# Three pairs of PSUM banks for the edge counts, and slot sums, block sums and turned features in the four partition groups of one bank

## What is computed

```python
def sage_conv(x, edge_index, W_l, b_l, W_r, num_segments):
    src, dst = (edge_index[0], edge_index[1])
    agg = jax.ops.segment_sum(x[src], dst, num_segments=num_segments)
    return agg @ W_l.T + b_l + x @ W_r.T
h = jax.nn.relu(sage_conv(x, edge_index, W_l_in, b_l_in, W_r_in, n))
out = sage_conv(h, edge_index, W_l_out, b_l_out, W_r_out, n)
x = _layernorm(x + out)
```

## Time and profile before

| | us |
|---|---|
| median of three executions | 5961.28 (5933.37 to 5972.20) |
| the profiled execution, its own time | 5973.71 |
| its span in the profile | 5971.6 |
| PE, ACT, DVE, POOL busy | 4194.8, 2238.6, 2727.6, 3172.5 |

### The profile page before, as it was taken

How to read it: one execution, slowest core, us unless ns; L and a number is a source line. 1 busy time by engine, 2 the same in 40 slices (tenths; PEclk the granted TensorE clock), 3 DMA queues, 4 the chain that set the end, 5 groups by cost and what they waited for, 6 DMA issues and landing times. The chain is left out here.

```text
span 5971.6 us, 92359 instructions
## 1 busy us (share of the span) xinstructions
PE 4194.8 (70%) x31126; PEld 3201.6 (54%) x31126; DVE 2727.6 (46%) x6953; ACT 2238.6 (37%) x5687; POOL 3172.5 (53%) x3030
## 2 busy tenths in 40 slices
PE   4777777777867777778757577676666676666656
PEld 2444444444445555544557566566565665566646
DVE  6635444444211111234322355655556556466586
ACT  2555555555300000156200045445454454444520
POOL 4645545555145555553066566565555655565645
PEclk9898888888667777888555567676677766667776
DMA  2323343343257777400122223333333333333332
GB/s 83 144 99 141 141 155 150 149 155 147 91 208 256 255 251 257 153 9 7 46 53 51 59 70 85 79 85 85 76 84 79 79 89 74 80 86 81 85 84 64
DMA packets 324619, 660.29 MB, mean 111 GB/s; under 512 B 124556, under 2 KB 208454, under 8 KB 316232
## 3 DMA queue, kind: packets, MB, share of 16 engines
q1 hardware_dynamic: 230246, 581.33, 27.6%
q0 software_dynamic: 92160, 74.67, 7.7%
q10 hardware_dynamic: 1896, 0.12, 0.0%
HBM read 393.69 MB, written 262.14 MB: 110 GB/s over the span
## 5 line engine op out<-in xcount | busy, mean ns | idle before, releaser
L1667 POOL DMA_INDIRECT gath<-fs_scratch,src_idx x1568 | 1615.4, 1030 | 1158.1 <-issue 459.9
L681 POOL DMA_INDIRECT gath<-in_x,src_idx x720 | 767.4, 1066 | 724.9 <-PE sum_x_ps_g L791 442.1
L1716 PE MATMUL ps_e<-fdw,scratch 128*128 128x66 f32 x3136 | 789.7, 337 | 395.8 <-issue 195.1
L729 ACT ACTIVATE scratch<-sum_x_ps_c 128x800 bf16<-128x800 f32 x932 | 763.0, 836 | 669.6 <-PE sum_x_ps_c L748 469.0
L1796 ACT ACTIVATE scratch<-scratch,bias,weight 128x32 f32<-128x32 f32 x2608 | 931.2, 403 | 55.1 <-DVE bias L1869 47.8
L1718 PE MATMUL ps_e<-gath,ident 128*128 128x66 f32 x3136 | 785.8, 336 | 151.4 <-issue 150.7
L681 POOL DMA_INDIRECT gath<-y_scratch,src_idx x592 | 597.2, 1009 | 543.1 <-PE sum_y_ps_g L791 353.2
L1716 PEld LDWEIGHTS ps_e<-fdw,scratch 128*128 128x128 f32 x3136 | 639.6, 249 | 454.5 <-issue 419.2
L1779 ACT ACTIVATE scratch<-ps_o 128x512 f32<-128x512 f32 x394 | 227.9, 596 | 1446.9 <-remote 844.8
L748 PE MATMUL sum_x_ps_c<-e_tab,scratch 128*128 128x400 bf16 x1864 | 541.2, 378 | 320.1 <-ACT scratch L729 171.2
L1718 PEld LDWEIGHTS ps_e<-gath,ident 128*128 128x128 f32 x3136 | 648.3, 252 | 161.6 <-issue 161.4
(11 more groups left out here) (276 smaller groups left out, 5308.2 us busy)
## 6 DMA issues: line engine op xcount, KB each, us to landing
count_scratch<-scratch SPq DMA_DIRECT2D x60, 3200.0 KB
scratch<-count_scratch SPq DMA_DIRECT2D x240, 800.0 KB
en_scratch<-gath SPq DMA_DIRECT2D x196, 264.0 KB
scratch<-en_scratch SPq DMA_DIRECT2D x196, 264.0 KB
scratch<-in_edge_attr_2x SPq DMA_DIRECT2D x390, 128.0 KB
gath<-fs_scratch,src_idx POOLq DMA_INDIRECT x1568
fdw<-fd_scratch SPq DMA_DIRECT2D x392, 33.0 KB
gath<-in_x,src_idx POOLq DMA_INDIRECT x720
```

The lines of the kernel that those rows point to most:

```text
L681: pool.indirect_dma_start(out=gath[:, s, t, 0:F], out_offset=None, in_=table_dram, in_offset=bass.IndirectOffsetOnAxis(ap=src_idx[:, g, k: ...
L729: act.activation(counts[:, b % 2, :, unit["column"]:unit["column"] + 2 * q] .rearrange("p a (h d) -> p h a d", h=2), ps_c[u % 2][:, :, 0:q ...
L1667: pool.indirect_dma_start(out=gath[:, s, t, :], out_offset=None, in_=fs_dram, in_offset=bass.IndirectOffsetOnAxis(ap=src_idx[:, g, k:k + 1 ...
L1716: pe.matmul(ps_e[g][:, k, 0:ROW], oht[:, s % 2, g * K + k, :], fdw[:, s, g, :], start=True, stop=False)
```

## The change

- The counts get three pairs of banks: unit u goes to `ps_c[u % 3]` and waits for `kept` of unit u-3.
- `ps_w` and the two `ps_g` go; one bank `ps_s` takes their place, with even slots in partitions 0:32, odd slots in 32:64, block sums in 64:96 and turned features in 96:128. PSUM is 6 + 1 + 1 banks.
- The table has the same four groups. An add waits only for adds into its own group.
- `w_in_t` holds the left weights three times and the right weights once, so the product between the passes takes 128 rows; the clears cover 96 rows.
- After sum_y the three groups are added by the matmul that turns them: an ordinary fp32 matmul of 96 rows with three identities stacked (`thrice`) in place of a transpose of 32 rows.

```diff
+        thrice = sb("thrice", [3 * F, F])
...
-                dve.tensor_copy(w_in_t[0:F, :], ps_w[0:F, 2, 0:HID])
-                dve.tensor_copy(w_in_t[F:2 * F, :], ps_w[F:2 * F, 2, 0:HID])
+                dve.tensor_copy(w_in_t[:, :], ps_w[:, 2, 0:HID])
+                for part in range(3):
+                    rows = slice(part * F, (part + 1) * F)
+                    dve.tensor_copy(thrice[rows, :], ident[rows, rows])
...
-                ps_c = [ctx.enter_context(nc.psum_tensor(f"{tag}_ps_c{i}", [P, 2, 512], F32)) for i in range(2)]
+                ps_c = [ctx.enter_context(nc.psum_tensor(f"{tag}_ps_c{i}", [P, 2, 512], F32)) for i in range(3)]
...
-                ps_w = ctx.enter_context(nc.psum_tensor(f"{tag}_ps_w", [2 * F, 512], F32))
-                ps_g = [ctx.enter_context(nc.psum_tensor(f"{tag}_ps_g{i}", [F, K, WINDOW], F32)) for i in range(2)]
+                ps_s = ctx.enter_context(nc.psum_tensor(f"{tag}_ps_s", [P, 512], F32))
...
+                def slot_sums(i, g):
+                    return ps_s[i % 2 * F:(i % 2 + 1) * F, g * WINDOW:(g + 1) * WINDOW]
...
-                            if u >= 2:
-                                pe.wait_ge(kept, u - 1)
+                            if u >= 3:
+                                pe.wait_ge(kept, u - 2)
...
-                            m = pe.matmul(ps_g[i % 2][:, t // K, :], gath[:, i % SLOTS, t, 0:F],
+                            m = pe.matmul(slot_sums(i, t // K), gath[:, i % SLOTS, t, 0:F],
...
-                            if tail:
-                                dve.wait_ge(tail_added, tail)
                             if b:
                                 dve.wait_ge(head_added, b)
-                            to = table_a[0:F, bass.ds(first, WINDOW)]
-                            dve.tensor_tensor(to, to, ps_w[0:F, 0:WINDOW], ALU.add).then_inc(head_added, 1)
-                            added = b + 1
+                            to = table_a[2 * F:3 * F, bass.ds(first, WINDOW)]
+                            dve.tensor_tensor(to, to, ps_s[2 * F:3 * F, 0:WINDOW], ALU.add).then_inc(head_added, 1)
...
-                                if tail:
-                                    dve.wait_ge(tail_added, tail)
-                                if added:
-                                    dve.wait_ge(head_added, added)
-                                to = table_a[0:F, bass.ds(starts[i % SLOTS * SG + g], WINDOW)]
-                                dve.tensor_tensor(to, to, ps_g[i % 2][:, g, :], ALU.add).then_inc(tail_added, 1)
-                                tail += 1
+                                if i >= 2 or g:
+                                    dve.wait_ge(tail_added, i * SG + g if g else (i - 1) * SG)
+                                to = table_a[i % 2 * F:(i % 2 + 1) * F, bass.ds(starts[i % SLOTS * SG + g], WINDOW)]
+                                dve.tensor_tensor(to, to, slot_sums(i, g), ALU.add).then_inc(tail_added, 1)
...
-                            t = pe.transpose(ps[:, c * K + k, :], table_a[0:F, c * GROUP + k:(c + 1) * GROUP:K],
-                                             ident[0:F, 0:F])
+                            t = pe.matmul(ps[:, c * K + k, :], table_a[0:3 * F, c * GROUP + k:(c + 1) * GROUP:K],
+                                          thrice[:, :], start=True, stop=True)
```

More of the change, by code:

```diff
@@ L244, in build @@
         attn_sb = sb("attn_sb", [P, HID])
-        w_in_t = sb("w_in_t", [2 * F, HID])
+        w_in_t = sb("w_in_t", [4 * F, HID])
+        thrice = sb("thrice", [3 * F, F])
         b_in = sb("b_in", [HID, 1])
@@ L366, in _ @@
                 pool.memset(trail[:, :], NOWHERE).then_inc(around_set, 1)
-                pool.memset(table_a[0:F, :], 0.0)
+                pool.memset(table_a[0:3 * F, :], 0.0)
                 pool.memset(column_i[:, :], 0).then_inc(pads_set, 1)
@@ L626, in _ @@
                 pe.wait_ge(w_loaded, 15 * 16)
-                pe.transpose(ps_w[0:F, 2, 0:HID], w_rows[0:HID, 0, 0:F], ident[0:HID, 0:HID])
-                pe.matmul(ps_w[F:2 * F, 2, 0:HID], w_rows[0:HID, 1, 0:F], ident[0:HID, 0:HID], start=True, stop=True)
+                for part in range(4):
+                    pe.matmul(ps_w[part * F:(part + 1) * F, 2, 0:HID], w_rows[0:HID, part // 3, 0:F],
+                              ident[0:HID, 0:HID], start=True, stop=True)
                 pe.transpose(ps_w[0:HID, 2, HID:HID + F], w_rows[0:F, 2, :], ident[0:F, 0:F])
@@ L717, in _ @@
                             act.wait_ge(turned, c + 1)
-                            act.activation(table_a[F:2 * F, c * GROUP:(c + 1) * GROUP]
+                            act.activation(table_a[3 * F:4 * F, c * GROUP:(c + 1) * GROUP]
                                            .rearrange("f (p k) -> f k p", k=K),
-                                           ps_w[F:2 * F, :].rearrange("f (k p) -> f k p", k=K), ACT.Copy)\
+                                           ps_s[3 * F:4 * F, :].rearrange("f (k p) -> f k p", k=K), ACT.Copy)\
                                .then_inc(placed, 1)
@@ L755, in _ @@
                             for k in range(K):
-                                m = pe.matmul(ps_w[F:2 * F, k * P:(k + 1) * P], values[:, c * K + k, :], ident[:, :],
+                                m = pe.matmul(ps_s[3 * F:4 * F, k * P:(k + 1) * P], values[:, c * K + k, :], ident[:, :],
                                               start=True, stop=True)
@@ L782, in _ @@
                                 pe.wait_ge(head_added, b)
-                            pe.matmul(ps_w[0:F, 0:WINDOW], sums[0:columns, b % 2, :], places[0:columns, b % 2, :],
+                            pe.matmul(ps_s[2 * F:3 * F, 0:WINDOW], sums[0:columns, b % 2, :], places[0:columns, b % 2, :],
                                       start=True, stop=True).then_inc(windowed, 1)
@@ L889, in done, with general_sum @@
             engine.wait_ge(sem, count)
-        def general_sum(tag, rows, table, slots, fill):
+        def general_sum(tag, rows, table, slots, fill, cleared):
             with ExitStack() as ctx:
@@ L946, in _ @@
                     with only_if_general(dve):
-                        done(dve, dve.memset(table[0:rows, :], 0.0), zeroed, 1)
+                        done(dve, dve.memset(table[0:cleared, :], 0.0), zeroed, 1)
                     def body(n, left):
@@ L1292, in _ @@
                     pool.wait_ge(h_summed, c + 1)
-                    pool.memset(table_a[0:F, c * GROUP:(c + 1) * GROUP], 0.0)
+                    pool.memset(table_a[0:3 * F, c * GROUP:(c + 1) * GROUP], 0.0)
             @block.sync
@@ L1304, in build @@
         segment_sum_pass("sum_y", y_dram, None, None, Plan(head, head.first_blocks, HB), False)
-        general_sum("all_y", F, table_a, E, gathering("all_y", y_dram, F))
+        general_sum("all_y", F, table_a, E, gathering("all_y", y_dram, F), 3 * F)
         early.close()
@@ L2049, in build @@
         general_softmax()
-        general_sum("all_m", HID, table_a, E, messages())
+        general_sum("all_m", HID, table_a, E, messages(), HID)
         with ExitStack() as ctx:
```

9 lines of the change are left out of this document (4 added, 5 removed).

## The result

| | before | after |
|---|---|---|
| median of 4 runs each (lowest to highest) | 5959.09 us (5933.37 to 5972.2) | 5879.69 us (5873.33 to 5886.59) |
| profiled execution, and its span | 5973.7, 5971.6 | 5874.28, 5872.2 |

The ratio is 0.9856 [0.9821, 0.9891]: faster by 1.4%. The forecast was 5886 us in a range of 5810 to 5985, and "faster by over 1%" had the greatest chance. The median before has a fourth execution in it; the forecast started from 5961.3 us.

A forecast was written before the change was run, and what follows sets the result against it. sum_x was taken as bound by PE's own work plus holds in front of units; 5973.7 - 110 (third pair) + 34.6 (turning) + 0.5 (set-up) = 5899 us profiled, median 5886 us, range 5810 to 5985.

The forecast's parts named there:

- The cause of the holds: sum_x: PE's completion signals come late while POOL gathers a slot, so PE waits; 318.9 us over 90 slots, 3.5 us each.
- Third pair: sum_x and counting part of sum_y: one PE step gained per hold, 91 us and 19 us, together 110 us less.
- Turning: Table turned back after sum_y: fp32 matmuls take 46.8 us instead of 12.2, 34.6 us more on the path.
- Split adds: DVE's table adds in both passes: waits for the other kind of add go; costed at nothing, covered by PE's idle time.
- A: Holds in both passes: PE's matmuls really held, not only signals; 88 us saved, net 53, time 5908; chance 0.13.
- B: Holds: PE waits for DVE's cells instead; 33 us back against 35 paid, time 5963; chance 0.15.
- C: Holds: fuller stretches keep PE at 2.4 GHz, each hold worth 1.91 us; 178 less 35, time 5818; chance 0.13.
- D: Bank ps_s: PE's writes wait while DVE or ACT reads, 155 us more, time 6041; chance 0.06.

## Why the prediction was right, point by point

**The cause of the holds: right as far as the gathers go.** "PE's completion signals come late while a slot is being gathered" rested on one timeline and a division by 90 slots. Without the gathers the holds are gone (waits for the copies 12.0 us for 211.5), and with the gathers spread they are smaller. That it is the signals which come late is not shown. The rows would look alike if the engines' own instructions reached them late, and PE's pauses ahead of products, which wait for nothing that the profile shows, speak for a part of that.

**Third pair, forecast 110 us: right in sum, measured 117 give or take 30.** In sum_x 107.5 us by the run with two pairs, where 91 were forecast; that the stage as a whole came out at -92 is luck, since 15.5 us of it went back (1492.5 us with two pairs, 1477 before). The composition was not as put, and the sign named for it was not met: the idle time ahead of the count matmuls was to shrink by a quarter or a third, and shrank by more than half (318.9 to 145.7), while that ahead of the products rose from 16 to 102. The forecast had one step of PE inside the hold; the step is there (the products of 797.03 to 799.72), but its eight products take 3 us for 0.5, and 102 us of waiting now stand ahead of the products. Another part came by way of the clock, 0.86 to 0.88, and PE's 20 us less of busy time. For the counting part 19 us were forecast and 25 seen, but only 333.7 - 323.4 = 10 of them go with the third pair, by the run with two pairs (its counting part is 333.7 us). The other 14 are in no term of the forecast; PE's own work there is 7 us less with two pairs already (269.5 for 276.8).

**Turning, forecast 34.6 us: right.** 46.85 - 12.17 = 34.7, and DVE's wait 39.94 for the 40 named. The value was taken from a row of the same kernel with the same shape at the same clock, against the bounds of 23 and 52. The clock stayed at 0.50, 1.2 GHz, for all of the 46.9 us in which PE was fully busy:

```profile
2710.40:2757.30 46.90, 46.79 (x200) 46.74 (x200) 6.99 (x2) 1.28 (x1) 0.00 (x0) 0.50 0.00 1
```

**Split adds, forecast nothing: too low, as far as can be seen.** "DVE has 791 us idle in sum_x and is a follower there." It is on average; yet cells, one-hots and sums are made by the same engine that is released late after each hold, and 12 us more of DVE's time there goes with 8 to 13 us more of the stage. The some 15 us in all lie inside the intervals. An engine's idle share says that there is room, not that the room is where the added work falls.

**What the forecast did not see: 24 us of the DRAM part.** Every profile with `ps_s` on the first two chips has 798 to 802 us there (after, two pairs, one table, spread gathers); the two with `ps_w` and `ps_g` have 822 (before) and 825 (turning alone). (On the third chip the changed kernel has 831.7 us, and no profile of the kernel before to set beside it.) PE's busy time falls by the same 23.6 us, with the same matmuls. A PE timeline shows where matmuls now lie over each other. First the kernel before, then the one after:

```profile
1727.99 0.41 PE L783 MATMUL sum_y_ps_w<-scratch 128*32 128x128 f32 x2
1728.23 0.38 PE L791 MATMUL sum_y_ps_g<-onehot,gath 128*32 128x128 f32 x2
```

```profile
1635.21 0.30 PE L790 MATMUL sum_y_ps_s<-scratch 128*32 128x128 f32 x1
1635.21 0.30 PE L798 MATMUL sum_y_ps_s<-onehot,gath 128*32 128x128 f32 x1
```

Before, a block sum (L783) and a slot's tile both go to partitions 0:32, and the tile starts 0.24 us later. After, the block sum goes to 64:96, the tile to 0:32 or 32:64, and both start at 1635.21. The Trainium skill, TensorE: Matmul & The Clock Gate (Part 3: Packing small matmuls — row/col tiling), says that matmuls at different tile positions of the array run concurrently; these two records agree. It is the partition group that does it, not the shared bank: in the kernel before with the block sums alone moved, banks as they were, the pair looks the same:

```profile
1402.03 0.30 PE L783 MATMUL sum_y_ps_w<-scratch 128*32 128x128 f32 x1
1402.03 0.30 PE L791 MATMUL sum_y_ps_g<-onehot,gath 128*32 128x128 f32 x1
```

In the DRAM part before there are 59 such places, and in 55 of them the tile starts 0.24 to 0.43 us behind the block sum (0.10 to 0.12 in four); in the profiles with the groups apart nine in ten or more start within 0.01 us. Added up the 59 delays are 18 us, an estimate of what the overlap can save. That it is worth 24 us of the kernel was not shown: both runs made for it fell where DMA hides it.

**The balance.** By stages, with the run with two pairs in between: the third pair gives -107.5 in sum_x, -10 in the counting part and -2 in the DRAM part; the shared bank and the split adds together +15.5, -14 and -22; the turning +35. That makes -106 us, beside -79 by the medians and -99 by the profiled executions. The forecast, -75, had the two large terms right and put the middle group, -21 in sum, at nothing.

**The rivals.** *A*, matmuls really held: its time, 5908, is not far off either, and size can't tell it from the forecast (it had 88 us for 110). The slow products of 797 to 800 speak for it in part, because PE itself crawls there; that the products of the step are all started before the release speaks for the forecast. It stays open how much is signals and how much matmuls. *B*, the cells as gate: fell; the waits named by the cells went from 58.9 to 37.0 us, not up. *C*, a gain by the clock: small, 0.86 to 0.88 in sum_x, where it needed over 0.9. *D*, one bank for three engines: fell. Adds and tiles that read and write `ps_s` take what they took in the earlier trace rows (the adds' median was 276 ns; the tiles' median is 297 ns in both kernels):

```profile
L872 DVE TENSOR_TENSOR table_a<-table_a,sum_x_ps_s x180: 267/280/283, 129.8 to 1455.5; 32x128 f32 x180
L798 PE MATMUL sum_x_ps_s<-onehot,gath x1440: 269/297/423, 99.7 to 1454.7; 128*32 128x128 f32 x180
```

## What to carry to other kernels

When several engines stop and start again together at regular places, look for a fourth that is busy only there, and take it away in an experiment before buying buffers: one more pair of banks bought one step for each hold (117 us), spreading the gathers took some 200 us more. Price an instruction by a row of the same kernel that has the same shape and clock, and look at its kind as well: an ordinary fp32 matmul took 0.47 us here where the transpose of the same data took 0.12. Test a gain on more than one chip: this one was 1.4% on one and 0.9% on another, and on a chip without holds the third pair gave 4 us of sum_x with the gathers left out.

## What the runs showed of the hardware that was not expected

- Chips of the same type differ by 30% on the same kernel: 5959, 5963 and 6054 us in three sets of runs, 4588 and 4579 on two other chips. The long ones are those where PE waits in sum_x while a slot is gathered: 211.5 us for the copies with two pairs, where the kernel with block sums in their own quadrant, also two pairs, has this on a chip without:

```profile
PE sum_x_ps_g L791 <- DMA gath<-in_x,src_idx: 44.7, 17, 7.3
...
PE sum_x_ps_c L748 <- ACT scratch L729: 8.7, 22, 1.3
```

  The waits in sum_x are not all of it: of the 1361 us between the profiles of the kernel before and of this one, 395 lie in sum_x, 266 in the DRAM part, 93 in the counting part and the rest behind them, where nobody looked. Whether this is the chip or its state at that hour was not settled; the one execution of 6051.03 us on a chip that otherwise takes 4600 may speak against a fixed property. The changed kernel as it is was not timed on a chip without holds.
- A hold outlasts the issue of its last gather by some two us, and it slows the start of matmuls that wait for nothing the profile shows. In the DRAM part of the kernel after, such products start in a beat: at 1600.23, 1601.64, 1603.05, 1605.87 and 1607.27, that is 1.4 or 2.8 us apart; the gaps inside the hold above are 0.55 to 0.73 us. The "issue" gaps of the DRAM part add up to 100.6 and 108.1 us ahead of the products of the kernel after, and are missing on the chips without holds:

```profile
PE sum_y_ps_d L779 <- issue: 108.1, 137, 2.6
PE sum_y_ps_c L779 <- issue: 100.6, 148, 2.6
```

- The holds cost twice: idle time of PE, and a lower clock. On chips with holds the clock granted in sum_x is 0.99 without gathers, 0.93 with spread ones, 0.85 to 0.88 with bursts; PE's busy time for the same 9624 matmuls is 954, 1017, and 1077 to 1125 us. On chips without holds it is 0.98 and 967 us with the gathers back to back (block sums alone).
